# A vision transformer tower on one core: the clip of attention's V from int16 to bf16, on GpSimd in place of VectorE

## What is computed

```python
def fake_quant(q, s, z):                      # QMAX = 15
    zr = ste_round(z)
    return s * (jnp.clip(ste_round(q / s) + zr, 0.0, QMAX) - zr)

qkv = fake_quant(x, sx1, zx1) @ fake_quant(ww1, sw1, zw1).T
q, k, v = map(split_heads, jnp.split(qkv, 3, axis=-1))
dots = einsum('bhnd,bhmd->bhnm', fake_quant(q, sq, zq), fake_quant(k, sk, zk)) * scale
a = softmax(dots, axis=-1)
out = einsum('bhnm,bhmd->bhnd', fake_quant(a, sa, za), fake_quant(v, sv, zv))
h = h + fake_quant(out, sx2, zx2) @ fake_quant(ww2, sw2, zw2).T + bb2
```

## Time and profile before

| | us |
|---|---|
| median of three runs | 1207.25 |
| the profiled execution, its time | 1207.43 |
| the profiled execution, span from the first to the last instruction | 1205.4 |
| TensorE busy | 1107.2 |
| VectorE busy | 1060.7 |
| ScalarE busy | 927.1 |
| GpSimd busy | 452.6 |

### The profile page before, as it was taken

One profiled execution on the slowest core, in us unless ns is written; L12 is line 12 of the kernel. 1 busy time (PEld: TensorE's weight loads), 2 busy tenths in 40 slices (PEclk: granted clock), 3 DMA queues, 4 the chain that ended last, 5 costly groups with the idle time before them and its releaser, 6 DMA issues.

```text
span 1205.4 us, 31929 instructions
## 1 busy us (share of the span) xinstructions
PE 1107.2 (92%) x11182; PEld 674.6 (56%) x11182; DVE 1060.7 (88%) x1979; ACT 927.1 (77%) x1877; POOL 452.6 (38%) x486
## 2 busy tenths in 40 slices
PE   7999999789999999999999999999748888888888
PEld 6999998345555555555555555555434444444444
DVE  7687576499999999999999999999978999999996
ACT  0000002779999999999999999999538999999997
POOL 5644343102211122322111232211237766666664
PEclk9999999989999999999999999999858999999999
DMA  8998997335555566555555666554432333333332
GB/s 292 327 305 256 313 299 219 121 127 144 154 151 149 148 135 152 150 147 152 158 145 150 136 147 153 152 152 140 132 104 72 99 99 98 98 98 98 98 93 70
DMA packets 158435, 187.86 MB, mean 156 GB/s; under 512 B 42864, under 2 KB 119808, under 8 KB 158080
## 3 DMA queue, kind: packets, MB, share of 16 engines
q1 hardware_dynamic: 117408, 158.10, 41.2%
q0 software_dynamic: 15360, 9.70, 8.9%
q10 hardware_dynamic: 25536, 18.31, 4.7%
HBM read 143.11 MB, written 36.12 MB: 149 GB/s over the span
## 4 chain that ended last, share of the span: by engine, by line
PE 63%; ACT 13%; issue 10%; DVE 5%; DMA 5%; SPq 2%; ACTq 0%; POOL 0%; DVEq 0%; POOLq 0%
PE psum L1118 14%; PE psum L1176 11%; PE psum L1239 11%; PE psum L1209 7%; PE psum L1179 6%; PE psum L1192 6%; PE psum L1226 5%; ACT ysq L685 3%; ACT yi L665 3%; ACT big L658 3%; DMA big<-z_row 2%; ACT zi L673 2%; ACT zT L643 1%; PE psum L1139 1%; DMA big<-xt 1%
## 5 line engine op out<-in xcount | busy, mean ns | idle before, releaser
L1051 DVE TENSOR_TENSOR pi<-big 128x2364 int16<-128x2364 f32 (+1 forms) x128 | 333.4, 2605 | 11.4 <-DMA big<-z_row 11.1
L754 POOL DMA_DIRECT2D h_res<-att x128 | 144.7, 1282 | 524.8 <-ACT att L598 515.6
L622 ACT ACTIVATE big<-psum 128x788 f32<-128x788 f32 (+1 forms) x384 | 330.1, 861 | 3.1 <-PE psum L1226 2.6
L584 ACT ACTIVATE qki<-psum 128x394 int16<-128x394 f32 x384 | 172.7, 510 | 26.1 <-PE psum L1179 13.9
L1118 PE MATMUL psum<-big 128*128 128x192 f32 (+1 forms) x1128 | 185.0, 327 | 1.3 <-DMA big<-xt 1.3
L1118 PEld LDWEIGHTS psum<-big 128*128 128x128 f32 (+1 forms) x1128 | 180.3, 188 | 4.4 <-DMA big<-xt 1.8
L1239 PE MATMUL psum<-big,sa_hot 128*32 128x197 f32 (+1 forms) x3072 | 169.6, 338 | 7.4 <-DVE zt L1075 7.4
L782 POOL TENSOR_TENSOR big<-big,goutb 128x512 f32<-128x512 f32 (+1 forms) x99 | 123.7, 1269 | 66.7 <-DVE big L1018 66.7
L584 ACT ACT_TABLE_LOAD x1 | 1.3, 1283 | 188.8 <-PE psum L1179 188.8
L1226 PE MATMUL psum<-qkb 64*128 64x197 bf16 (+1 forms) x1536 | 129.5, 247 | 0.3 <-DVE qkb L843 0.3
L593 ACT ACTIVATE vi<-psum 128x384 int16<-128x384 f32 (+1 forms) x256 | 115.4, 528 | 12.4 <-PE psum L1179 12.2
(11 more groups left out here) (106 smaller groups left out, 1803.7 us busy)
## 6 DMA issues: line engine op xcount, KB each, us to landing
big<-z_row SPq DMA_DIRECT2D x192, 394.0 KB, 5.0
big<-xt SPq DMA_DIRECT2D x98, 384.0 KB, 4.6
tin<-h_res SPq DMA_DIRECT2D x49, 192.0 KB, 3.0
tres<-h_res SPq DMA_DIRECT2D x49, 192.0 KB, 2.5
out<-oo SPq DMA_DIRECT2D x49, 192.0 KB, 2.6
h_res<-big ACTq DMA_DIRECT2D x84, 96.0 KB, 4.4
h_res<-att POOLq DMA_DIRECT2D x64, 96.0 KB, 3.3
x_int<-big ACTq DMA_DIRECT2D x84, 64.0 KB, 4.3
```

The costliest lines, as they stand in the source:

```text
L584: act.activation(qki[:, k, :, :], psum[:, bank, 0:2 * N] .rearrange("p (c n) -> p c n", c=2), ACT.Copy, scale=factor[(F_Q, F_K)[b % 2]])\
L622: act.activation(ex[0:r, tri, t, 4 * g:4 * g + 4, :].rearrange("p (a h) n -> p a h n", a=2), psum[0:r, 2 * t:2 * t + 2, 0:2 * N] .rearrang ...
L754: pool.dma_start(h_res[bass.ds(b - 4, 1), t0:t0 + r, :].rearrange("a n d -> (a n) d"), att[0:r, par, t, :], accum_op=ALU.add).then_inc(s_a ...
L1051: v.tensor_tensor(pi[0:r, t, :, 0:N], ex[0:r, it, t, :, :], zb[0:r, ip, :, :], ALU.mult).then_inc(s_pi, 1)
```

## The change

The clip of V leaves VectorE's list and is written at the head of GpSimd's `image_step`, with the same two waits and the same semaphore `s_vb` at its end. The buffers, the consumer (`weighted_values`) and ScalarE's wait stay as they are. From the function on GpSimd the lines below move down by 5.

```diff
 (GpSimd, image_step)
                 if b == 4:
                     for p in range(2):
                         pool.wait_ge(s_h1[p], stores_at(LAST - (LAST - p) % 2))
+                if has_unit(b, -U1):
+                    pool.wait_ge(evac["v"], 4 * b)
+                    wait(pool, full["o"], 3 * (b - 3))
+                    nc.gpsimd.tensor_scalar(vb[:, (tri + 2) % 3, :, :], vi[:, 1 - par, :, :], lo[:, ZV:ZV + 1],
+                                            hi[:, ZV:ZV + 1], ALU.max, ALU.min).then_inc(s_vb, 1)
                 if has_unit(b, -4 * U1):
                     wait_apart(pool, evac["y"], b - 3)
...
 (VectorE, image_step)
                 if has_unit(b, -3 * U1):
                     clip_probs(b - 3, nxt, 1)
-                if has_unit(b, -U1):
-                    dve.wait_ge(evac["v"], 4 * b)
-                    wait(dve, full["o"], 3 * (b - 3))
-                    clip(vb[:, (tri + 2) % 3, :, :], vi[:, nxt, :, :], None, 128, ZV).then_inc(s_vb, 1)
                 if has_unit(b, -4 * U1):
                     dve.wait_ge(evac["o"], 3 * b - 9)
```

## The result

| | before | after |
|---|---|---|
| median of the runs (four of each) | 1207.84 | 1496.87 |
| lowest and highest of the runs after | | 1496.23, 1501.31 |
| the profiled execution, its time | 1207.43 | 1497.29 |
| GpSimd busy | 452.6 | 790.0 |
| VectorE busy | 1060.7 | 1277.0 |

The ratio is 1.2393 [1.2376, 1.241]: slower by 289 us, where the prediction had 10 and a range that ended at 1263. The sign was right and the size was wrong by far.

A forecast was written before the change was run, and what follows sets the result against it. TensorE and ScalarE were taken to set 10.06 us per image, VectorE a close third. Held VectorE adds 12.5 us, less 1.6 of lag not paid, 0.46 and 0.1: +10.3, forecast 1217.5 us, range 1204.5 to 1263.

The forecast's parts named there:

- What bounds the kernel: Attention images: TensorE and ScalarE, waiting for each other's PSUM banks, set 10.06 us; VectorE, needing 9.77, is a close third.
- 1.6: Microseconds gained by taking V's clips off VectorE: 0.46 before the first steady step, 2 x 0.59 at the end.
- the 0.88 us: Blocking per image (10.06 - 9.18) under which VectorE, without V's clip, still keeps up.
- Where the clip lands: On GpSimd behind the two adding DMAs, beginning 0.2 to 0.35 us ahead of VectorE's probability multiply.
- That a running GpSimd operation holds the multiply: Through the shared SBUF port, GpSimd's clip shuts out VectorE's probability multiply, for its duration less 0.25 us.
- The clip then takes 1.60 us: Duration of V's clip on GpSimd, taken from the rate of a one-input copy; the low end.
- The bound from above, 3.44: High end in microseconds for V's clip on GpSimd, at the two-input add's rate.
- The hold, 1.1 us: GpSimd's clip delays VectorE's probability multiply by 1.35 - 0.25 us per image; bounds 0.2 and 2.9.
- ScalarE's deadline: ScalarE needs the clip done before writing a later image's V into the same buffer, 5.62 us after att.
- The rival that has ScalarE waiting for V: Clip starts after the multiply and ends late for ScalarE: 1280 us, or near 1500 behind the second multiply; chance 0.10.
- VectorE then needs 9.18 + 1.1 = 10.28 us, 0.22 more than 10.06; over 57 images 12.5 us: Main term: VectorE, relieved of V's clip but with its multiply held, becomes the attention images' bound; chance 0.48.

The follow-up runs named there:

- e10: The changed kernel with no clip of V at all, vb a constant and GpSimd only raising the semaphore; 1205.42 us, ratio 0.9987.
- e9: The changed kernel with GpSimd's clip cut to an unbounded conversion of half of V, the other half of vb constant; 1207.6 us, ratio 1.0006.
- e1: The kernel before with eleven GpSimd operations behind its last output, VectorE done; clip 5.53 us, one arithmetic operation 4.15, copy 1.46, two-input add 3.41.
- e2: The changed kernel with a third vi buffer, so ScalarE needs the clip one image later; 1490.98 us, ratio 1.2301.
- e3: The kernel before, VectorE still clipping V, plus a same-size GpSimd clip that nobody reads or waits for; 1499.04 us, ratio 1.2304.
- e5: The changed kernel with GpSimd's clip replaced by a plain conversion without bounds, 1.46 us by itself; 1261.24 us, ratio 1.0447.
- e4: The kernel before, with ScalarE's vi also waiting for five small GpSimd powers (26 elements) whose output is unused; 1736.86 us, ratio 1.4357.
- e7: The kernel before, with ScalarE's vi also waiting for three small GpSimd powers (16 elements) whose output is unused; 1584.08 us, ratio 1.3133.

## Why the prediction was right in sign and wrong in size

- **What bounds the kernel: right.** TensorE and ScalarE set 10.06 us and VectorE has little to spare. e10 took 2.2 us off where the prediction had 1.6, and e9 stayed at no change below the 0.88 us.
- **Where the clip lands: right.** Behind the DMAs and just ahead of the multiply (0.08 us by their end, at 612.27 against 612.35).
- **That a running GpSimd operation holds the multiply: right.** No row of before showed it; now it is 6.69 us against 2.58. The rule of the Trainium skill, page "SBUF — State Buffer", section "Who interferes with whom", holds here in that direction as well. (That the rows of before agreed "for the clips in both directions" was said too much: they have an add holding a clip and a multiply holding a GpSimd operation, but no clip holding one.)
- **"The clip then takes 1.60 us": the step that failed.** It is 5.53 us alone. The bound from above, 3.44, was no bound either: it assumed that one input cannot cost more than two, while e1 shows that the two arithmetic operations of the clip cost more than a second input does. The row that was nearest was not the copy but the multiply by a per-partition scalar, 331 ns for three elements, which is too small to give a rate. The Trainium skill, page "GPSIMD Engine Reference", section "4.1 Engine selection", calls one-input work on GpSimd roughly line-rate; e1 agrees for the copy and the conversion (1.46 us), and not for the clip.
- **The hold, 1.1 us: followed the clip.** With the measured clip it is 3.9 us on the multiply (mean 6.46, 300 to 900 us), so VectorE needs 9.18 + 3.9 = 13.1 us. That is under 14.7: in the kernel after VectorE is not the bound, and it waits for TensorE. What was not thought of is that the hold can move to the clip of the second half (e2, e3, e5).
- **ScalarE's deadline: right, and it was the loop to follow.** The 5.62 us after `att` are missed once the clip exceeds about 5.62 - 0.79 - 1.86 - 0.1 = 2.9 us. The rival that has ScalarE waiting for V came near in number (1500) but for another reason: it had the clip lose its place to the multiply, while in the kernel after the clip keeps its place and is long. That number was luck.
- **TensorE's clock: missing.** Nothing in the working let TensorE slow down after a wait. That is 1.8 of the 4.65 us per step.
- **"VectorE then needs 9.18 + 1.1 = 10.28 us, 0.22 more than 10.06; over 57 images 12.5 us": also wrong, by less.** e5 shows that with nearly the duration assumed the loss is 54 us (1261.24 - 1207.25) and not 10. The hold was 1.36 in place of 1.1, and the lag that it builds up moves the hold onto the second half's clip, where TensorE pays 3.5 us at once.

What stays open: how the loss would split if only one limit were half removed (the hold alone gives nearly all of it in e3; for the wait alone the chain of the kernel after says so, in which VectorE has 1%, and e4 and e7 with longer waits; so the two overlap and don't add), and whether another place for the clip, ahead of the DMAs for instance, would hide more; it wasn't tried.

## What to carry to other kernels

Price an operation that moves to another engine by a row of the same operation with the same number of arithmetic steps on that engine, at a size that gives a rate; a copy says nothing of a clip on GpSimd (1.46 against 5.53 us). Then follow its end to whoever waits for it, and ask by how much it may be late, before costing what it does to others: here 2.9 us was the limit. Where an engine shares a port with a nearly saturated one, the hold lands on whatever that engine runs at that moment, and the dearest place is the instruction that a third engine waits for.

## What was not expected of the hardware

- GpSimd's two-bound clip releases VectorE at different times. If the multiply, once released, took its usual 2.58 us, it ran on from 612.35 + 6.69 - 2.58 = 616.46 us, 1.4 us before the clip's recorded end (617.85). The clip of the second half, held by the same operation in e2, ran on only 0.27 us before that end (0.25 us in the earlier trace rows).
- The hold on the clip of the second half is longer than the operation that holds it. In e2 it starts at 603.13, 0.17 us before GpSimd's clip by the record and 0.80 before the DMA in front ends, and takes 7.01 us: 6.1 of hold by an operation of 5.6. In e5 it starts at 624.64, 0.32 us before the conversion, and is held by 2.2 us, where the conversion takes 1.46 by itself. The DMA alone does not hold it: in the kernel before it starts at 504.15, inside the DMAs of 503.64 to 507.10, and takes 0.90 us. Why it is shut out so early stays open.
- TensorE, idle for 2.78 us in the step shown, ran at the upper level for some time after it and then at the lower one: 1.00, 0.80 and 0.50 in three stretches of the timeline one after the other (616 to 618 us, where it was idle, 618 to 620, 620 to 622). After 2.15 us idle in the next step it stayed at 1.00.
- Five powers of 26 elements took 9.38 us in one step of e4 and 10.22 in the next, where the kernel before has 1.35 us in the mean for a power of six; that mis-sized e4 and e7. VectorE holding GpSimd in return, as in the earlier trace rows, would explain it; no run tests that.
